# Second attention of a fused transformer block: value parts directly ahead of the scores, and one copy by ACT of a pair's first projection

## The reference, cut to what matters

```
xn = layernorm(x)                      # (4, 512, 256)
q = (xn @ Wq) -> (b, h, 512, 64)       # four heads
k, v = split(context @ Wkv)            # (b, h, 1024, 64) each
attn = softmax(q k^T * 64**-0.5)       # (b, h, 512, 1024), mask given
x = x + (attn @ v -> (b, 512, 256)) @ Wo
```

## Time and profile before

| | us |
|---|---|
| median of 3 runs | 965.04 (962.65 to 968.49) |
| the profiled execution, its own time | 967.79 |
| span of its instructions | 965.9 |
| second attention, first scores to the last output projection on PE | 384.10 to 641.75 |
| PE busy over the span | 894.5 (93%) |

### The profile page before, as it was taken

How to read it: one execution, slowest core, us unless ns; L and a number is a source line. 1 busy time by engine, 2 the same in 40 slices (tenths; PEclk the granted TensorE clock), 3 DMA queues, 4 the chain that set the end, 5 groups by cost and what they waited for, 6 DMA issues and landing times. The chain is left out here.

```text
span 965.9 us, 19473 instructions
## 1 busy us (share of the span) xinstructions
PE 894.5 (93%) x6189; PEld 766.2 (79%) x6190; DVE 562.0 (58%) x1286; ACT 491.3 (51%) x1044; POOL 431.3 (45%) x374
## 2 busy tenths in 40 slices
PE   6899999868999998779999999988899999999995
PEld 4798989746899996557777777757499999999995
DVE  7875453485566675666566575554764454454452
ACT  5744141354444553475665665545655455455552
POOL 2474341004555573755363462300255555555543
PEclk9999999978999999789999999985999999999998
DMA  9721000275766746611010100019667666676662
GB/s 306 239 95 44 1 1 1 76 248 187 254 228 232 253 157 221 135 44 44 5 63 22 45 1 2 28 52 353 229 184 195 211 200 190 209 203 187 206 198 28
DMA packets 68593, 134.72 MB, mean 139 GB/s; under 512 B 8080, under 2 KB 50704, under 8 KB 63408
## 3 DMA queue, kind: packets, MB, share of 16 engines
q1 hardware_dynamic: 55184, 110.27, 33.4%
q0 software_dynamic: 13344, 23.63, 11.2%
HBM read 109.08 MB, written 21.64 MB: 135 GB/s over the span
## 5 line engine op out<-in xcount | busy, mean ns | idle before, releaser
L1901 PEld LDWEIGHTS d_hps<-d_xg_t,d_xw 128*128 128x128 f32 x1248 | 145.2, 192 | 2.4 <-DVE d_xg_t L2085 1.0
L1799 ACT ACTIVATE x<-d_hps,b 128x128 f32<-128x128 f32 x312 | 89.3, 368 | 113.1 <-PE d_hps L1901 112.9
L1901 PE MATMUL d_hps<-d_xg_t,d_xw 128*128 128x128 f32 x1248 | 145.5, 275 | 0.8 <-DVE d_xg_t L2085 0.8
L883 POOL TENSOR_SCALAR c_prob<-c_prob,c_rinv 128x1024 f32<-128x1024 f32 x64 | 72.4, 1150 | 109.4 <-DVE c_rinv L1338 109.0
L1911 PE MATMUL d_yps<-d_w,d_hid_hi 128*128 x312 | 115.2, 402 | 0.0
L1704 POOL DMA_INDIRECT out_x<-d_y,d_take_slot x39 | 63.1, 1619 | 99.1 <-DVE d_y L2122 89.6
L1331 DVE CUSTOM_DVE_ANT_0 c_prob<-c_sc,c_minf 128x1024 f32<-128x1024 f32 x64 | 75.8, 1221 | 36.6 <-PE c_sc L976 34.4
L2085 DVE TENSOR_SCALAR d_xg_t<-d_take,ln_w,ln_b 128x128 f32<-128x128 f32 x78 | 28.5, 406 | 93.4 <-PE d_take L1890 93.1
L1914 PE MATMUL d_yps<-d_w,d_hid_lo 128*128 x312 | 81.2, 281 | 0.0
L1901 PEld LDWEIGHTS b_hps<-b_xg_t,b_w 128*128 128x128 f32 x624 | 76.7, 195 | 3.6 <-issue 1.9
L989 PE MATMUL c_tp<-const,c_prob 128*128 128x128 f32 x512 | 70.5, 281 | 9.8 <-DVE c_pt L1343 5.2
(11 more groups left out here) (367 smaller groups left out, 2106.6 us busy)
## 6 DMA issues: line engine op xcount, KB each, us to landing
d_xw<-in_w SPq DMA_DIRECT2D x39, 1024.0 KB
b_w<-in_w SPq DMA_DIRECT2D x47, 512.0 KB, 7.6
d_w<-in_w SPq DMA_DIRECT2D x8, 1024.0 KB, 12.3
a_raw<-in_ctx_t SPq DMA_DIRECT2D x8, 512.0 KB, 7.0
a_raw<-in_ctx SPq DMA_DIRECT2D x8, 512.0 KB, 4.6
ybuf<-a_zero SPq DMA_DIRECT2D x2, 2048.0 KB, 12.5
k_stage<-in_ctx_t SPq DMA_DIRECT2D x12, 256.0 KB, 3.0
rows<-b_xn_all SPq DMA_DIRECT2D x1, 2048.0 KB, 12.6
```

What stands on the lines that cost most here:

```text
L883: nc.gpsimd.tensor_scalar(prob[w][:], prob[w][:], rinv[:, w:w + 1], 1.0, ALU.mult, ALU.mult).then_inc(s["prob_ready"], 1)
L1799: op = nc.scalar.activation(hid[q][:, h * FH + c, :], src[:, c, :], ACT.Gelu_apprx_tanh, bias=b1[:, ds(e, 1), h * FH + c])
L1901: mm = nc.tensor.matmul(hps[j % 2][h][:, c * P:(c + 1) * P], w1[j % WL][:, k, at:at + P], xg_t[j % 2][:, k, :], start=(k == 0), stop=(k == ...
```

## The change

It has two parts, both in `attention1`.

1. Value parts are moved. Each now stands directly ahead of a `scores`, and the places between two `turn` and between a `turn` and a projection, where they stood, are left empty. Their waits follow (c_v_in, and c_att_ready one step stricter). ACT's `keep_heads` and some of its other steps are reordered to match. The order of DVE's and POOL's steps is the same, except for the low parts below.
2. For the k projections and the transposed xn, ACT first copies the first of a pair from c_xb to a new SBUF buffer c_held (`hold`). The second of the pair waits for this copy alone (c_held) instead of DVE's low part. The high and low parts of the first are then made from c_held, behind the exponentials and the first high-half copy. The buffer is taken from c_gap, so no other tile moves.

The output projection is not copied: its second half still waits for DVE (c_x_ready). The q projection has no pair and is not copied either.

```diff
+        held = sb("held", [P, S])
-        sb("gap", [P, 5248])
+        sb("gap", [P, 4736])
@@ values(b, m, part)
-                if part == 0 and b * 4 + m >= 2:
-                    pe.wait_ge(s["att_ready"], b * 4 + m - 1)
+                pe.wait_ge(s["v_in"], b * 4 + 2 * part + 2)
+                if part == 0 and b * 4 + m:
+                    pe.wait_ge(s["att_ready"], b * 4 + m)
@@ tensor: units 0 and 1
+                if before:
+                    values(b - 1, 2, 0)
                 scores(b, 0)
                 if before:
                     k_proj(1, 0, xb[:])
                     turn(b - 1, 7, 0)
-                    values(b - 1, 2, 1)
-                    pe.wait_ge(s["k_lo"], b * 4 + 3)
+                    pe.wait_ge(s["held"], b * 3)
                     k_proj(1, 1, xb[:])
                     turn(b - 1, 7, 1)
+                if before:
+                    values(b - 1, 2, 1)
                 scores(b, 1)
                 pe.wait_ge(s["k_lo"], b * 4 + 4)
                 q_proj(1, xb[:])
...
                 turn(b, 0, 0)
+                turn(b, 0, 1)
                 if before:
                     values(b - 1, 3, 0)
-                turn(b, 0, 1)
-                if before:
-                    values(b - 1, 3, 1)
                 scores(b, 2)
@@ tensor: units 4 to 7
+                values(b, 0, 0)
+                scores(b, 4)
...
                 if before:
...
                     project(b - 1, 0, xb)
                 turn(b, 3, 0)
-                values(b, 0, 1)
                 if before:
                     pe.wait_ge(s["x_ready"], b * 2 - 1)
                     project(b - 1, 1, xb)
                 turn(b, 3, 1)
+                values(b, 0, 1)
                 scores(b, 5)
...
+                values(b, 1, 1)
                 scores(b, 7)
                 if more:
                     pe.wait_ge(s["k_lo"], b * 4 + 6)
                     q_proj(0, xb[:])
+                else:
+                    values(b, 2, 0)
                 turn(b, 6, 0)
-                values(b, 2, 0)
                 turn(b, 6, 1)
@@ scalar
+            def hold(done, n, freed, count):
+                act.wait_ge(s[done], n)
+                act.wait_ge(s[freed], count)
+                nc.scalar.activation(held[:], xb[:], ACT.Copy).then_inc(s["held"], 1)
...
                 if before:
-                    k_high(b, 1, 0, xb[:])
+                    hold("k_done", b * 4 + 3, "k_lo", b * 4 + 1)
                 keep_and_exp(b, 0)
                 if before:
-                    keep_heads(b - 1, 2)
+                    from_held(b * 3)
+                    k_high(b, 1, 0, held[:])
                     k_high(b, 1, 1, xb[:])
@@ vector
                 both_maxima(b, 6)
-                if more:
-                    k_low(b + 1, 0, 0, xb[:])
                 keep_and_inverse(b, 6)
                 if more:
+                    k_low(b + 1, 0, 0, held[:])
                     k_low(b + 1, 0, 1, xb[:])
```

More of the change, by code:

```diff
@@ L1034, in tensor @@
                 before, more = b > 0, b < B - 1
-                if not before:
+                if before:
+                    values(b - 1, 2, 0)
+                else:
                     pe.wait_ge(s["k_lo"], 4)
@@ L1069, in tensor @@
                 if before:
+                    values(b - 1, 3, 1)
+                scores(b, 3)
+                if before:
                     pe.wait_ge(s["v_in"], b * 4 + 2)
                     v_proj(2, xb[:])
-                scores(b, 3)
+                turn(b, 2, 0)
                 if before:
@@ L1076, in tensor @@
                     v_proj(3, xb[:])
-                turn(b, 2, 0)
+                turn(b, 2, 1)
+                values(b, 0, 0)
+                scores(b, 4)
                 pe.wait_ge(s["v_in"], b * 4 + 4)
-                values(b, 0, 0)
-                turn(b, 2, 1)
-                scores(b, 4)
                 if before:
@@ L1100, in tensor @@
                 turn(b, 4, 0)
-                values(b, 1, 0)
                 if more:
-                    pe.wait_ge(s["xn_lo"], b * KD + KD + 1)
+                    pe.wait_ge(s["held"], b * 3 + 1)
                     turn_x(1, xb)
                 turn(b, 4, 1)
+                values(b, 1, 0)
                 scores(b, 6)
@@ L1123, in tensor @@
                     q_proj(0, xb[:])
+                else:
+                    values(b, 2, 0)
                 turn(b, 6, 0)
-                values(b, 2, 0)
                 turn(b, 6, 1)
+            values(B - 1, 2, 1)
             turn(B - 1, 7, 0)
-            values(B - 1, 2, 1)
-            turn(B - 1, 7, 1)
             pe.wait_ge(s["att_ready"], B * 4 - 1)
@@ L1133, in tensor @@
             project(B - 1, 0, xb)
+            turn(B - 1, 7, 1)
             values(B - 1, 3, 0)
@@ L1218, in scalar @@
                 if before:
-                    k_high(b, 1, 0, xb[:])
+                    hold("k_done", b * 4 + 3, "k_lo", b * 4 + 1)
                 keep_and_exp(b, 0)
                 if before:
-                    keep_heads(b - 1, 2)
+                    from_held(b * 3)
+                    k_high(b, 1, 0, held[:])
                     k_high(b, 1, 1, xb[:])
                     keep_first(b - 1, 7, 1)
+                if before:
+                    keep_heads(b - 1, 2)
                 q_high(b, 1, xb)
@@ L1228, in scalar @@
                 keep_first(b, 0, 1)
-                if before:
-                    keep_heads(b - 1, 3)
                 if before:
@@ L1240, in scalar @@
                 if before:
+                    keep_heads(b - 1, 3)
                     keep_v(b, 2, xb[:])
+                keep_first(b, 2, 0)
+                exponentials(b, 3, 0)
+                if before:
                     keep_v(b, 3, xb[:])
-                keep_and_exp(b, 3)
+                exponentials(b, 3, 1)
                 keep_first(b, 2, 1)
@@ L1261, in scalar @@
                         x_norm(b + 1, t)
+                if b == 0:
+                    act.wait_ge(s["sum_d3"], 16)
+                keep_heads(b, 0)
                 if more:
-                    x_high(b + 1, 0, xb)
+                    hold("xn_tp", b * KD + KD + 1, "k_lo", b * 4 + 3 if before else 0)
                 keep_and_exp(b, 5)
                 if more:
+                    from_held(b * 3 + 1)
+                    x_high(b + 1, 0, held)
                     x_high(b + 1, 1, xb)
@@ L1273, in scalar @@
                 if more:
-                    k_high(b + 1, 0, 0, xb[:])
+                    hold("k_done", b * 4 + 5, "xn_lo", b * KD + KD + 1)
                 keep_and_exp(b, 6)
-                keep_heads(b, 1)
                 if more:
+                    from_held(b * 3 + 2)
+                    k_high(b + 1, 0, 0, held[:])
                     k_high(b + 1, 0, 1, xb[:])
                 keep_first(b, 5, 1)
+                keep_heads(b, 1)
                 if more:
@@ L1284, in scalar @@
                 keep_first(b, 6, 1)
+            keep_heads(B - 1, 2)
             keep_first(B - 1, 7, 0)
-            keep_heads(B - 1, 2)
             keep_first(B - 1, 7, 1)
@@ L1394, in vector @@
                 both_maxima(b, 0)
-                if before:
-                    k_low(b, 1, 0, xb[:])
                 keep_and_inverse(b, 0)
                 if before:
+                    k_low(b, 1, 0, held[:])
                     k_low(b, 1, 1, xb[:])
```

13 lines of the change are left out of this document (5 added, 8 removed).

## The result

The changed kernel takes 978.27 us (median of 6 runs, 971.83 to 985.59), the kernel before 964.68 in the runs taken beside them (6 runs, 960.47 to 968.49): a ratio of 1.0147, 95% interval 1.0093 to 1.0201. It is slower by 13.6 us; the prediction said 11.3, and 976.3 us in a range of 970.5 to 983.5. The profiled execution took 982.8, its span is 980.5.

What follows compares the result with a forecast made beforehand. The prediction took PE to bound the kernel, nearly full from batch 1 on. Stalls of 6.9, 3.6, 1.9 and 1.7 us less a gain of 2.8 gave +11.3, so 965.04 became 976.3 us, range 970.5 to 983.5.

Steps and rivals of the forecast that it cites:

- What a switch costs, and the gain: PE's group switches: entering a value part or scores costs about 0.11 us, leaving a value part 0.06; gain 2.8 us.
- The row of before: PE's trace before the change: value part straight into scores takes 1.87 us, with no visible cost for changing tiling mode.
- The copy by ACT at nothing: Second k projections: ACT's 9 extra copies of 0.60 us into c_held lie in its idle time and cost nothing.
- The q units, 1.15 each: Six units with a q projection: PE stands 1.15 us for DVE's copy before the second turn's high half; 6.9 us.
- Batch 3, units 5 and 6, 1.8 each: Two turns directly after the scores wait for DVE's copy: 7.32 us per unit against 5.52, together 3.6 us.
- The output projection, 0.64 each: Its second half waits for DVE to add the first to x: 0.64 us in three batches, 1.9 us.
- Batch 0, 1.7 with bounds 0.3 and 3.7: Units 3 to 5: a value part moves behind the wait for outside sums, at low clock; 1.7 us lost.
- Rival (a), the clock: Batch 3, units 5 and 6: stalls lower the granted clock, 3.5 us each time, giving 979.8 to 983.3; chance 0.17.
- the prediction's own sign of being wrong: The forecast counts as wrong if, among other signs, the granted clock falls below 1.00 in batches 1 to 3.
- The sum: Whole kernel: 6.9 + 3.6 + 1.9 + 1.7 - 2.8 = +11.3 us, to 976.3 us.

Runs made afterwards that it cites:

- Experiment 7: The changed kernel with unit 5's value part in batches 0 to 2 back between the first turn and the second transposed xn; 974.61 us.
- experiment 8: The changed kernel run once more, with nothing altered; 978.81 us, ratio 1.0124 to the kernel before.
- experiment 9: The changed kernel with c_held placed behind c_gap in SBUF and no other edit; 983.98 us.
- experiment 4: The changed kernel with the value parts of units 4 and 5 of batch 0 back ahead of the wait for the sums; 980.54 us, ratio 1.0187.
- experiment 1: The changed kernel with the value part back between the two turns at six places in units with a q projection; 972.33 us, ratio 1.010.
- experiment 2: The changed kernel without ACT's copy into c_held, so PE waits for DVE's low part again; 985.74 us, ratio 1.0252.
- experiment 6: The kernel before with only the value parts of units 5 and 6 of batch 3 moved behind both turns; 973.81 us.
- experiment 5: The changed kernel with value parts moved only where covered, and DVE's first projection addition between unit 4's maxima; 961.45 us, ratio 0.9973.

## Why the prediction was right, and where it was off

- **What a switch costs, and the gain.** Predicted 2.8 us, 1.1 of them in each full batch. Batches 1 and 2 grew by 2.9; their losses (two q units 2.38, the output projection 0.65, unit 5 1.03) add up to 4.06, so the gain is 1.17 each. Batch 3 grew by 4.80 with losses of 5.58, a gain of 0.8 where the prediction had 0.5. In all that is 3.2. Of the 32 value parts 28 now go straight into scores: 26 take 1.87 to 1.88 to the start of the scores, and the other two, 3.54 and 3.61, are those at the low clock in batch 0. The row of before was the right thing to go by.
- **The copy by ACT at nothing.** Right: no wait for c_held, and 8.7 us worse without it.
- **The q units, 1.15 each.** Measured 1.19 at six places, 7.1 for 6.9. The chain of starts on DVE came out to 0.01 us.
- **Batch 3, units 5 and 6, 1.8 each.** Measured 3.92 for two turns that cost 2.05 with a value part between them, so 1.87 each, 3.7 for 3.6.
- **The output projection, 0.64 each.** Projection at 491.87, turn at 493.70, second projection at 495.20: the turn takes 1.50 instead of 0.85, 1.9 for 1.9. DVE's addition starts at +2.59, as in the earlier trace rows.

```profile
491.87 1.99 PE L1012 MATMUL c_xb<-c_wo,c_att_t 128*128 128x256 f32 x8
493.70 1.04 PE L990 MATMUL c_tp<-const,c_prob 128*128 128x128 f32 x8
495.20 1.99 PE L1012 MATMUL c_xb<-c_wo,c_att_t 128*128 128x256 f32 x8 [0.46 <-DVE x L1374]
```

- **The step that was missed: unit 5 of batches 0 to 2.** The prediction's part on the gain gave every unit one turn at 0.86 and one at 0.97, and its part on the costs looked for stalls in units with a q projection, without a projection, and with an output projection. Unit 5 has a projection of its own kind, the transposed xn, whose group is only 0.49 us long. A k or v projection of 1.5 us on each side of the first turn is cover for DVE's two maxima; 0.49 is not. PE, then DVE:

```profile
501.46 0.66 PE L931 MATMUL c_xb<-const,k_rows 128*128 128x128 f32 x4
501.95 1.04 PE L990 MATMUL c_tp<-const,c_prob 128*128 128x128 f32 x8
502.82 0.63 PE L931 MATMUL c_xb<-const,k_rows 128*128 128x128 f32 x4
503.38 0.63 PE L990 MATMUL c_tp<-const,c_prob 128*128 128x128 f32 x4
504.79 0.66 PE L990 MATMUL c_tp<-const,c_prob 128*128 128x128 f32 x4 [0.78 <-DVE c_pt L1368]
505.37 1.95 PE L1003 MATMUL c_av<-c_pt,c_v 128*64 128x256 f32 x16
```

```profile
501.75 1.23 DVE L1356 CUSTOM_DVE_ANT_0 c_prob<-c_sc,c_minf 128x1024 f32<-128x1024 f32 x1 [2.96 <-PE c_sc L977]
...
504.05 0.69 DVE L1368 COPY c_pt<-c_tp 128x512 f32<-128x512 f32 x1
```

  The second turn takes 505.37 - 503.38 = 1.99 us instead of 0.97. That is 1.0 us in three batches, **3.1 us** that the sum lacked. PE's half could start 0.49 + 0.87 + 0.56 + 0.43 = 2.35 after the unit's transposed xn, and DVE's copy ends 3.3 after it (504.05 + 0.68 - 501.46); the prediction's own figures, 0.46 to 0.49 for the transposed xn and +3.26 for the copy behind two maxima, would have told it. Experiment 7 took 0.8 of it away per batch, by a place that costs a value part's exit again.
- **Batch 0, 1.7 with bounds 0.3 and 3.7.** In the three profiles of this order (the changed kernel, experiments 8 and 9) batch 0 takes 69.43, 67.21 and 66.22 us, in two of the order of before 64.36 and 64.47. Less the q unit (1.19) and unit 5 (1.03) of this batch and with its gain of 0.1, the rest is 3.0, 0.7 and -0.3, in the mean 1.1. The term holds in the mean, but its spread is as large as its bounds. Over units 3 to 5 alone the three profiles take 22.39, 19.70 and 19.65 us; they differ in PE's wait for ACT's copy behind the sums (2.80, 1.31 and 1.43) and in how long the two value parts and the scores behind them ran at the low clock. The eleven profiles beside experiment 4 give 2.1 us for this stretch, where the prediction had 2.0 before it took 0.3 off.
- **Rival (a), the clock.** The prediction gave 0.17 to it. Of eight profiles with the full stalls of units 5 and 6 in batch 3 (the changed kernel and experiments 1, 2, 4, 6, 7, 8 and 9) three show the fall, each time once, behind unit 5, and worth about 1.6 us, and five don't. It is a part of the scatter of this kernel, at half the price that was set for it, and it was underrated: 3 in 8. By luck the profile of the changed kernel is without it; its repeat (experiment 8) meets the prediction's own sign of being wrong, a granted clock below 1.00 in batches 1 to 3. What decides whether it falls was not tested.
- **The sum.** With measured sizes: 7.1 + 3.7 + 1.9 + 3.1 + 1.1 - 3.2 = 13.7 us, and 1.6 more where the clock falls. The attention is longer by 15.7, 15.1 and 14.3 us in the three profiles, and the medians differ by 13.6. The predicted 11.3 is 2.4 below this sum. Unit 5 alone is 3.1 short; batch 0 (1.1 for 1.7) and the gain (3.2 for 2.8) took 1.0 of that back by luck.
- **Outside the attention** two profiles may not be compared. What stands ahead of the attention is not touched and ended between 363.8 and 374.7 us over all profiles (364.4 before, 369.0 after). The first stretch behind it took 57.8 us before and 51.9 after, and 49.4 to 58.0 over all. That range goes with the granted clock there, which was 0.50 from 647 to 680 in the kernel before and 1.00 here up to 683.5:

```profile
668.00:683.50 15.50, 13.66 (x109) 11.57 (x109) 11.69 (x30) 11.65 (x16) 0.00 (x0) 1.00 0.95 294
```

  The changed kernel run again (experiment 8) had the low clock there and 58.0 us. So the difference of the spans (14.6) is not the attention's alone: +15.7 in it, +4.6 ahead, -5.9 behind, 0.2 elsewhere. What sets that clock was not tested.

## What to carry to other kernels

Work placed between two uses of a single buffer is cover for whoever empties that buffer. Before moving it, go through every place with the same question: when does the emptying engine's list reach the copy, counted from a start that both engines share, and how much does the waiting engine have in hand by then? Do it for each kind of unit, also for the one whose groups are short; the unit left out here cost 3.1 us, more than the sum's whole error. The small costs between groups (0.06 to 0.11 us) are worth a move only where the cover stays: 14 stalls of 0.6 to 1.9 us, 15.8 us together, stand against a gain of 3.2.

## What the runs showed of the hardware

DVE's subtraction `c_k_lo<-c_held,c_k_hi` took 1.51 us, twice the 0.68 of the same operation with c_xb (PSUM) as input, and `c_xn_lo<-c_held,c_xn_hi` of the same form took 0.69. POOL tells them apart. Its row in the changed kernel, two scalings of 1.12 us each, and DVE's beside it:

```profile
447.00 2.25 POOL L884 TENSOR_SCALAR c_prob<-c_prob,c_rinv 128x1024 f32<-128x1024 f32 x2 [0.54 <-DVE c_rinv L1363]
```

```profile
448.28 1.51 DVE L1342 TENSOR_TENSOR c_k_lo<-c_held,c_k_hi 128x512 fp32r<-128x512 f32 x1 [0.36 <-ACT c_k_hi L1174]
449.71 0.68 DVE L1342 TENSOR_TENSOR c_k_lo<-c_xb,c_k_hi 128x512 fp32r<-128x512 f32 x1
```

POOL's second scaling ends at 447.00 + 2.25 = 449.25, and DVE ends 0.54 later. The same pair in experiment 5, where DVE began later in POOL's instruction (first POOL, then DVE):

```profile
502.25 2.66 POOL L884 TENSOR_SCALAR c_prob<-c_prob,c_rinv 128x1024 f32<-128x1024 f32 x2
```

```profile
502.98 0.94 DVE L1351 TENSOR_TENSOR c_k_lo<-c_held,c_k_hi 128x512 fp32r<-128x512 f32 x1 [0.36 <-ACT c_k_hi L1183]
```

The first scaling ends at 502.25 + 1.12 = 503.37 or so; DVE ends at 503.92, again 0.55 later, and the two scalings take 2.66 instead of 2.25: the second one waited in turn. Over the 18 such subtractions in the two kernels, of both kinds, the eleven that began 0.1 to 0.2 into a scaling took 1.51 to 1.53, the two that began 0.4 before its end 0.93 and 0.94, and the five that began 0.1 before its end took 0.69 and left the next scaling at about 1.6. One `c_xn_lo<-c_held,c_xn_hi` in experiment 5 is among the eleven, so it is not the pair of operands either. So with two inputs in SBUF, DVE and POOL exclude each other for a whole instruction. The Trainium skill, "SBUF — State Buffer", section "SBUF: two separate sides", says so: a DVE instruction with two SBUF inputs and a GpSimd one that reads SBUF take a shared pair of ports as an exclusive lock. The trace agrees, and c_xb as one input is free of it (0.68 at 503.85 in experiment 5, beside POOL's second scaling). It costs this kernel nothing visible, since PE waits for nothing behind these subtractions; but copying a PSUM tile to SBUF first, as this change does, turns the low part from an instruction that does not wait for POOL here into one that does.
